# Two recurrent layers of attention and routed experts: the shared experts of layer 0 in weight-stationary chunks, half of them beside the first projections

## The reference, cut to what matters

```python
x = L0_attn_x                                 # (4, 256, 256) float32: 1024 tokens, 8 tiles of 128
xn = _layernorm(x)
s = _L0_attn_ref(xn, ...)                     # differential attention, 16 heads x 2 maps
g = _silu(_L0_ffn_ref(xn, ...))
x = x + s * g
xn = _layernorm(x)
s = _L1_attn_ref(xn, ...)
g = _silu(_L1_ffn_ref(xn, ...))
x = x + s * g

def _L0_ffn_ref(x, gate_w, w1, w2, w3, sw1, sw2, sw3):
    # _swiglu(t, wa, wb, wo): h = silu(t @ wa.T) * (t @ wb.T); return h @ wo.T
    scores = softmax(t @ gate_w.T)            # 16 experts, INTER = 176
    weights, indices = top_k(scores, 2)
    for e in range(16):
        y = y + _swiglu(t, w1[e], w3[e], w2[e]) * w_e[:, None]
    z = _swiglu(t, sw1, sw3, sw2)             # shared experts, 2 x 176 wide, for every token
    return y + z
```

## Time and profile before

| | |
|---|---|
| median of 3 runs | 543.9 us (542.84 to 544.36) |
| profiled execution: its time, its span | 546.77 us, 545.0 us |
| TensorE busy | 440.9 us, 81% of the span |
| VectorE busy | 325.9 us, 60% |
| ScalarE, GpSimd busy | 188.7 and 184.8 us |
| mean granted TensorE clock | 0.902 |
| layer 0 attention, experts of layer 0, layer 1 | about 0 to 228, 228 to 350, 350 to 545 us |

### The profile page before, as it was taken

The page is one execution under the profiler, slowest core; times in us unless marked ns, Lnnn a source line. Parts: engine busy times, 40 slices in busy tenths (PEclk is TensorE's granted clock), DMA queues, the critical chain, the costliest instruction groups (busy, mean ns, idle before and its releaser), DMA issues.

```text
span 545.0 us, 10275 instructions
## 1 busy us (share of the span) xinstructions
PE 440.9 (81%) x3600; PEld 305.3 (56%) x3600; DVE 325.9 (60%) x831; ACT 188.7 (35%) x407; POOL 184.8 (34%) x224
## 2 busy tenths in 40 slices
PE   3456898878898998799999999765594969889960
PEld 2324666544574564477776776553573646577640
DVE  3786647799887765135331338788569566732335
ACT  1101324443444555633453323121103333454212
POOL 2333200353786214004000047243606385411324
PEclk9857979999999999999999999889567989899985
DMA  7340775466496520413332253033623747000114
GB/s 230 95 122 2 232 225 164 139 200 200 124 292 192 158 55 3 135 60 98 108 106 70 77 188 102 10 92 112 176 86 100 220 150 229 27 2 14 62 34 144
DMA packets 50492, 65.87 MB, mean 121 GB/s; under 512 B 8051, under 2 KB 41715, under 8 KB 48907
## 3 DMA queue, kind: packets, MB, share of 16 engines
q1 hardware_dynamic: 48139, 58.93, 35.5%
q0 software_dynamic: 2304, 6.29, 3.6%
HBM read 42.88 MB, written 22.02 MB: 119 GB/s over the span
## 4 chain that ended last, share of the span: by engine, by line
PE 54%; DVE 21%; POOL 7%; issue 6%; DMA 5%; SPq 3%; ACT 2%; POOLq 0%; DVEq 0%; ACTq 0%
PE bank L1010 9%; PE bank L1032 7%; PE bank L905 4%; DVE work L1471 4%; PE bank L912 4%; PE bank L808 3%; PE bank L839 3%; DMA work<-work 3%; PE bank L955 3%; PE bank L933 3%; PE bank L835 3%; POOL x_slots L1297 2%; DVE work L1435 2%; PE bank L793 2%; PE bank L1017 2%
## 5 line engine op out<-in xcount | busy, mean ns | idle before, releaser
L1471 DVE TENSOR_REDUCE work<-bank 128x4 f32<-128x512 f32 (+1 forms) x144 | 96.3, 687 | 61.1 <-PE bank L839 59.2
L1133 ACT ACTIVATE work<-bank 128x512 f32<-128x512 f32 x144 | 84.1, 595 | 105.7 <-PE bank L863 61.8
L835 PE MATMUL bank<-neg_ts,identb 128*128 128x512 bf16 (+1 forms) x144 | 49.2, 341 | 30.8 <-DVE work L1471 24.5
L1097 ACT ACTIVATE work<-bank 128x256 f32<-128x256 f32 (+4 forms) x131 | 51.5, 401 | 60.3 <-PE bank L905 20.7
L1261 POOL TENSOR_TENSOR work<-work 128x512 f32<-128x512 f32 (+1 forms) x20 | 21.3, 1064 | 109.4 <-ACT work L1097 109.2
L912 PE MATMUL bank<-work,cst 128*32 128x256 f32 (+1 forms) x768 | 52.7, 345 | 0.0
L905 PE MATMUL bank<-work 128*32 128x128 f32 (+1 forms) x704 | 49.0, 352 | 3.9 <-POOL work L1252 2.6
L1774 DVE TENSOR_TENSOR work<-work,bank 128x176 f32<-128x176 f32 x47 | 15.8, 336 | 59.6 <-ACT work L1186 59.3
L839 PE MATMUL bank<-work 96*128 96x256 bf16 (+1 forms) x320 | 50.2, 262 | 0.0
L1032 PE MATMUL bank<-moe,work 88*128 (+1 forms) x188 | 50.2, 390 | 0.0
L1010 PE MATMUL bank<-moe,work 128*128 x124 | 42.1, 462 | 0.8 <-ACT work L1097 0.5
(11 more groups left out here) (196 smaller groups left out, 772.9 us busy)
## 6 DMA issues: line engine op xcount, KB each, us to landing
moe<-w_in SPq DMA_DIRECT2D x27, 352.0 KB, 3.9
work<-q_parts SPq DMA_DIRECT2D x48, 128.0 KB, 2.6
x_slots<-wo SPq DMA_DIRECT2D x9, 512.0 KB, 3.9
work<-x_slots SPq DMA_DIRECT2D x31, 128.0 KB, 2.2
y_slots<-work SPq DMA_DIRECT2D x31, 128.0 KB, 1.7
q_parts<-work SPq DMA_DIRECT2D x8, 384.0 KB, 2.7
parts<-work SPq DMA_DIRECT2D x8, 384.0 KB, 2.8
moe<-parts SPq DMA_DIRECT2D x24, 128.0 KB, 2.6
```

Source lines behind the costliest of these rows:

```text
L835: nc.tensor.matmul(view[:, :, half * P:half * P + P], identb[:, :], neg_ts[:, :].unsqueeze(1).to_broadcast([P, len(ms), P]), start=True, s ...
L1097: return nc.scalar.activation(dst, src, ACT.Copy)
L1133: nc.scalar.activation(pT[at % 6], a.st.bank(w)[:, :], ACT.Exp, scale=SCALE)\
L1471: nc.vector.tensor_reduce(here[:, first:first + len(ms), half], a.s.bank((b, q))[:, :].rearrange("p (m s) -> p m s", s=n), AX_X, ALU.max, ...
```

## The change

The shared experts become chunks of work on a pair of tiles (256 tokens). Chunk c of pair g is one half (88 of 176 columns) of one shared expert: TensorE multiplies with the weights as the stationary operand (`shared_up`: 4 products of 256 columns, first and third matrix side by side in one PSUM bank), ScalarE takes the silu of one half of the bank, VectorE multiplies it by the other, and the result, already turned, is the stationary operand of `shared_down` (2 products of 256 columns), which adds up all four chunks of a pair in one bank. The transposes of the hidden rows, the copies of them, and the adds into `acc` go away for the shared experts; ScalarE copies the finished bank.

Pairs 0 and 1 (`AHEAD = 2`, tiles 0 to 3) are put on layer 0's line of beats: pair 0 at beats 7 to 13, pair 1 at beats 18 to 27, with PSUM banks 4 to 7 that the exponentials need later. Their results are stored to a DRAM tensor (`shared0`) and loaded into `acc` during the third routed tile. The shared weights are loaded at the start, behind the masks and ahead of the second half of x, and leave the bulk list (35 loads instead of 38); the first bulk load of `w2` waits for both stores, as the parked results use its place. Pairs 2 and 3 remain in the expert loop as 8 rounds (31 to 38). The loop has 50 rounds instead of 53, the combinations stand in rounds 37 to 44, and layer 1's first steps start at round 42 instead of 44. The silu of the gate is written in place (`acc` for `gval`), and some loads share a semaphore.

```diff
+         bulk=(30, 2), shared=(((7, 8, 9), (8, 9, 10), (9, 10, 11), (10, 11, 12), 13),
+                                ((18, 19, 20), (20, 21, 22), (22, 23, 24), (24, 25, 26), 27)),
...
-         early=(44, 0, 3, 4, 4, 5, 9, 9, 10)),
+         early=(42, 0, 3, 4, 4, 5, 9, 9, 10)),
...
+CHUNKS = 2 * SHARED
+COMBINE = (6, 7, 8, 9, 10, 11, 12, 13)
+ROUNDS0 = 50
...
+            for g, at in enumerate(c.get("shared", ())):
+                for k, (up, hidden, down) in enumerate(at[0:CHUNKS]):
+                    put(up, "shared_up", CHUNKS * g + k)
+                    put(hidden, "shared_hidden", CHUNKS * g + k)
+                    put(down, "shared_down", CHUNKS * g + k)
+                put(at[CHUNKS], "shared_out", g)
...
+        sh.up = Ring(banks[4:7], sem("sh_up_full"), dve=sem("sh_hidden"))
+        sh.bank = banks[7]
...
-            return [t for t in range(TILES) if max(SLOT_TILES0 + 7 + t, SLOT_TILES0 + 4 + 2 * t) + lag == n]
+            return [t for t, at in enumerate(COMBINE) if SLOT_TILES0 + at + lag == n]
...
-        N0 = SLOT_TILES0 + SHARED * TILES
+        N0 = SLOT_TILES0 + CHUNKS * (TILES // 2 - AHEAD)
...
             sp.dma_start(masks, consts_d[:, C_KEPT:C_TABLES]).then_inc(ld["cst"], 16)
+            sp.dma_start(w13[:, E0:], w13_d[:, E0:]).then_inc(ld["shared"], 16)
+            sp.dma_start(w2[0:FH, E0:], w2_d[:, E0:]).then_inc(ld["shared"], 16)
             for g in range(2, TILES // 2):
                 x_pair(g)
...
+                    elif kind == "shared_out":
+                        sp.wait_ge(sh.out, w + 1)
+                        sp.dma_start(shared_d[w * SEQ:(w + 1) * SEQ, :].rearrange("(t p) d -> p t d", p=P),
+                                     early_out.rearrange("p (t d) -> p t d", d=D)).then_inc(sh.kept, 16)
...
                 if n == 3:
                     sp.dma_start(x_again, x_d.rearrange("(t p) d -> p t d", p=P)).then_inc(ld["x2"], 16)
+                    sp.dma_start(acc[:, 0:2 * AHEAD, :], shared_d.rearrange("(t p) d -> p t d", p=P)).then_inc(ld["x2"], 16)
...
+                if a.n == 0 and key == (0, 0, 0):
+                    sh.up.wait_drained(pe)
+                    pe.wait_ge(sh.out, AHEAD)
...
+            def shared_up(bank, k):
+                g, c = divmod(k, CHUNKS)
+                part, f = divmod(c, 2)
+                for u in range(2):
+                    col = u * F0 + f * FH
+                    for d in range(KD):
+                        mm = nc.tensor.matmul(bank[0:FH, u * SEQ:(u + 1) * SEQ], w13[:, E0 + part, d, col:col + FH],
+                                              xnT[:, d, 2 * g:2 * g + 2, :], start=(d == 0), stop=(d == KD - 1))
+                return mm
+
+            def shared_down(bank, hidden, k):
+                part, f = divmod(k % CHUNKS, 2)
+                for u in range(2):
+                    mm = nc.tensor.matmul(bank[:, u * D:(u + 1) * D], hidden[0:FH, k % 3, u * P:(u + 1) * P],
+                                          w2[0:FH, E0 + part, f, :], start=(k % CHUNKS == 0 and u == 0),
+                                          stop=(k % CHUNKS == CHUNKS - 1), skip_group_check=True)
+                mm.then_inc(sh.down, 1)
...
+                    elif kind == "shared_up":
+                        if w == 0:
+                            pe.wait_ge(ld["shared"], 32)
+                        pe.wait_ge(*a.pj.emptied(("x", w // CHUNKS)))
+                        sh.up.wait_free(pe, w)
+                        shared_up(sh.up.bank(w), w).then_inc(sh.up.full, 1)
+                    elif kind == "shared_down":
+                        if w % CHUNKS == 0 and w:
+                            pe.wait_ge(sh.out, w // CHUNKS)
+                        pe.wait_ge(*sh.up.emptied(w))
+                        shared_down(sh.bank, early_hidden, w)
...
+            def shared_silu(bank, hidden, k):
+                if k >= 3:
+                    act.wait_ge(sh.down, k - 2)
+                nc.scalar.activation(hidden[0:FH, k % 3, :], bank[0:FH, 0:SEQ], ACT.Silu).then_inc(sh.silu, 1)
...
+                    elif kind == "shared_out":
+                        if w:
+                            act.wait_ge(sh.kept, 16 * w)
+                        act.wait_ge(sh.down, CHUNKS * (w + 1))
+                        copy(early_out, sh.bank[:, :]).then_inc(sh.out, 1)
...
+            def shared_hidden(ring, key, hidden, k):
+                dve.wait_ge(sh.silu, k + 1)
+                half = hidden[0:FH, k % 3, :]
+                nc.vector.tensor_tensor(half, half, ring.bank(key)[0:FH, SEQ:2 * SEQ], ALU.mult).then_inc(ring.free["dve"], 1)
...
-                    if j < SLOT_TILES0:
-                        if j >= 4:
-
-                            dve.wait_ge(ys_stored[j % 4], 16 * (j // 4))
-                        nc.vector.tensor_copy(ys[:, j % 4, :], src).then_inc(m0.dn.free["dve"], 1)
-                    else:
-                        t, part = divmod(j - SLOT_TILES0, SHARED)
-                        if part == 0:
-                            nc.vector.tensor_copy(acc[:, t, :], src).then_inc(m0.dn.free["dve"], 1)
-                        else:
-                            dve.wait_ge(*m0.dn.emptied(j - 1))
-                            nc.vector.tensor_tensor(acc[:, t, :], src, acc[:, t, :], ALU.add).then_inc(m0.dn.free["dve"], 1)
+                    if j >= 4:
+
+                        dve.wait_ge(ys_stored[j % 4], 16 * (j // 4))
+                    nc.vector.tensor_copy(ys[:, j % 4, :], m0.dn.bank(j)[:, 0:D]).then_inc(m0.dn.free["dve"], 1)
```

165 lines of the change are left out of this document (98 added, 67 removed).

## The result

The changed kernel takes 553.3 us (median; 551.95 to 556.18) against 544.1 for the kernel before in the same session: ratio 1.0158, 95% interval 1.0121 to 1.0194. Run again in a later session, beside e9, e11 and e12, it was 1.0115 (1.0041 to 1.0189). The forecast was 542.5 with a range of 536.5 to 549.0: it missed, in sign too. The profiled execution took 551.95 (span 550.1), 5.2 above the profiled one of before (546.77).

The account below looks back on a forecast made before the run. TensorE was taken to bound the late expert stage, VectorE the time after 345 us. The terms -9.3 + 1.2 + 7.0 + 0.5 - 0.8 = -1.4 us took the median 543.9 to 542.5, range 536.5 to 549.0.

Parts of the forecast that it names:

- The late stage, -9.3: Late experts to layer 1's first row maximum: removed shared rounds and waits bring that maximum 9.3 us sooner, at 376.9.
- Its cold projections: Late stage: idle TensorE starts layer 1's transposes and first projection at the low clock, a new wait of +3.0 us.
- Pair 0, +1.2: Layer 0, beats 7 to 13: VectorE's multiplies and a silu wait delay the first row maximum 1.2 us, to 34.75.
- Pair 1, +7.0: Layer 0's row maxima, beats 18 to 27: TensorE's strict order delays batch 1's first turn by 7.0 us more, to 52.7.
- clock, +0.5: Layer 0's row maxima: TensorE's clock may relapse after a thin stretch; one relapse costs 1.7 us, taken as +0.5.
- rival 1: Layer 0: row maxima take pair 1 in back to back, +3.4 us for all early cost, total 537.2; chance 0.15.
- Loads, -0.8: Three fewer bulk loads end before the fourth batch's maxima rows, which land faster: 0.8 us saved, bounds 0 and -1.1.
- Acc fetch, table loads, parked rows: 0: Fetching parked results during the third routed tile and ScalarE's table switches beside layer 0's exponentials are covered: 0 us.
- rival 5: ScalarE among layer 0's row maxima: a silu comes late behind its table loads; chance 0.03.
- The signs listed beforehand: Observations that would confirm the forecast: TensorE without early hole, landmark times in both layers, granted clock near 1.
- rival 4: Layer 1's first steps: VectorE and GpSimd contend more, only 6.4 us come back late, total 545.4; chance 0.08.
- bound of -7.1: Late stage: the smallest gain the forecast allowed, 7.1 us, beside -15 as the largest.

Follow-up runs that it names:

- e9: Changed kernel with half-size fillers (unused TensorE products in the late stage) and the last normalisation ahead of the second projections' turns: ratio 0.9986 to the kernel before.
- e11: Changed kernel with no pair early, all sixteen shared chunks in the expert loop, last normalisation moved ahead, second batch's rows four rounds later: ratio 1.0030 to the kernel before.
- e12: Changed kernel with pair 1's four down products one beat later: ratio 1.0016 to the kernel before.
- e6: Changed kernel with the last two tiles' normalisation ahead of the second projections' turns on VectorE: ratio 1.0050 to the kernel before.
- e5: Changed kernel with half-size fillers (18, 15 and 9 unused TensorE products) in the late stage's idle stretches: ratio 1.0062 to the kernel before.
- e14: Changed kernel with pair 1's downs one beat later, the last normalisation moved ahead and half-size late fillers of TensorE: ratio 0.9880 to the kernel before.
- e2: Changed kernel without pair 1's four early chunks, rows of x standing in for their results: ratio 1.0002 to the kernel before.
- e1: Changed kernel without any early chunk, rows of x standing in for the parked results: ratio 0.9952 to the kernel before.
- e13: Changed kernel with pair 1's downs one beat later and the last normalisation ahead of the second projections' turns: ratio 0.9933 to the kernel before.
- e15: Changed kernel with both pairs' downs one beat later and the last normalisation ahead of the second projections' turns: ratio 0.9917 to the kernel before.
- e10: The changed kernel, unaltered, run again in a later session: ratio 1.0115 to the kernel before.
- e18: The kernel before, unaltered, run once more for a second trace: layer 1's first row maximum at 388.08 us, against 386.17 in its first trace.

## Why the prediction was wrong, point by point

- **The late stage, -9.3: this step failed.** It gave 2.6 in the profiled pair, and 2.6 to 4.9 over the traces. The first half of it held: the gathers gate the first norm, which ended 1.1 us later relative to the first expert round (0.8 forecast). What failed is the stretch behind it: 38.1 us, where the sum said 34.0 and I took 31.8. By rows: VectorE waits 5.8 us for projections (the sum left 3.0), and the last normalisation takes 4.5 beside GpSimd (1.5 in the operations of before). Together that is 5.8 us more, of which some 1.7 net came back elsewhere: the waits for GpSimd's powers (1.2 in the earlier trace rows) are gone and fewer combinations and gates meet GpSimd, but a second normalisation meets it too (3.1 us from 368.47 on). The other 2.2 were the choice of the lower of two sums "as the groups count overlapped ends twice". I had added up "with as much contention as those of before show", and the normalisations among those, three in the earlier trace rows, ran without company; the one at 28.50 in the same trace had it. An operation's company is a property of when it runs, and the change moved it. e6 shows it: with the normalisation out of that company and inside a wait, the stretch is 33.4, between the two sums.
- **Its cold projections.** The forecast had them (+3.0) and gave them to the first projection only; the second ones ran cold as well (TensorE idle 8.0 us before the second pair's transposes and 5.7 before its projections). e5 gets part of the second wait, e14 nothing more: it is one wait, which either a warm clock or other work of VectorE fills. The first wait stays at 3 us in all of them.
- **Pair 0, +1.2:** 1.4 at the first maximum in the changed kernel's trace (0.5 to 2.4 over all kernels with pair 0 early), and 2.7 in time (e2 against e1). Mis-sized: the wait for the last silu was named but not priced apart, and there was no term for the clock behind a pair that is done early (0.50 from 37.0 to 47.2 in e2). What moves the first maximum by over a microsecond between versions with the same pair 0 is open.
- **Pair 1, +7.0:** 7.7 at the turn, 6.2 to 8.5 in time, so the walk through the order was right, with TensorE's two waits of 0.77 us and the three ups, downs and products as listed. (Layer 0 as a whole, 7.9 in the forecast, is 8.3 in this pair of traces but 7.9 to 10.9 over all of them, so the close agreement is in part luck.) The **clock, +0.5,** was one relapse at 38.8 to 42.2, just where the text put it: 3.4 us at a granted clock of 0.50, so 1.7 lost, and the weight was too small. (The 1.7 us that the forecast gave one relapse rest on no row of the kernel before. Its trace has the clock at 0.50 for 3.4 us from 175.5 on, but also for 20.5 from 21.9 on, and e2 for 10.2: that the run showed just 1.7 is luck.) What the walk didn't ask is whether the price belongs to the work or to its order; the lower bound that it named (turn at 47.9, rival 1) is a beat away (48.95 in e12).
- **Loads, -0.8:** e1, which keeps the changed order of loads, has its turn 0.60 us later than before and its first expert round 0.79 later (229.43 against 228.64): no gain that reaches the experts.
- **Acc fetch, table loads, parked rows: 0.** Held. In ScalarE's timeline of the kernel after, the table loads between silu 5 and 6 took 1.28 us each, the exponential began 0.02 behind the first, and no multiply waited for them. Silu 6 began at 47.60, 1.10 behind the second load and released by TensorE, so the case of rival 5 (0.03), a silu late behind its tables, did not come:

```profile
43.70 1.28 ACT L1196 ACT_TABLE_LOAD   x1
45.00 0.20 ACT L1196 ACTIVATE small<-small 128x2 f32<-128x2 f32 x1
45.22 1.28 ACT L1176 ACT_TABLE_LOAD   x1
```

- **The signs listed beforehand.** No hole of TensorE from 16 to 30: held, though narrowly (e13 and e15, with the same loads, wait 0.31 and 0.95 us for the shared weights there). First maximum near 34.8 (34.97), gathers 0.8 later relative to the experts (1.3), turn near 53 (54.89): near. Clock near 1 from 39 to 55: 0.50 up to 42.2, then 1.00. Layer 1's first maximum 9 us sooner relative to the experts: 2.6. Sooner by 6 was the sign of rival 4, contention of VectorE and GpSimd as the steps close up. It named the right mechanism, at 0.08, and less than half of the shortfall (2.9 of 6.7); the bound of -7.1 on the late term was no bound, since it held contention at the level of before.
- **A count in parentheses.** For a pair of tiles the forecast set 6,144 columns against 5,888 of the old rounds. In passes, as it counts elsewhere, they are 12,288 and 10,752: the new form costs TensorE 10.3 us for a pair where the old one cost 9.0. No other number rests on it.
- **What stays open.** The profiled executions differ by 5.2 us, the medians by 9.1 at first and by 6.7 (ratio 1.0115) later. The changed kernel's median is the same in both sessions (553.3 and 553.2); that of before was 544.1, from four executions, and 545.1 to 546.5, from 13 to 31, in all later sessions. So part of the first 9.1 lies in those four. The steps above explain the profiled pairs (5.1 us of span at first, 5.4 for e10 against e18); where the rest lies no run shows.

## What to carry to other kernels

When work leaves an engine, sum the engine that stays, operation by operation and with its neighbours at their new times: here VectorE took seven times as long for a small step beside GpSimd (1.11 us against 0.16), and moving one normalisation was worth as much as the work that left. When work is put among the steps of a chain, ask what the order alone costs, by giving every product one more step before its consumer: here one beat was worth as much as six of the eight us that the work seemed to cost. Here the freed engine also ran at a lower clock (0.68 against 0.84 in the last stretch); try filling the waits that this causes with other work before warming it.

## What the runs showed of the hardware

Steps of VectorE on 128x2 elements that ran 0.16 us alone took 1.07 and 1.11 in the kernel after beside GpSimd's operations and ended with them to 0.02 us; one of before, at 28.50, took 1.02 and did the same. Row maxima that read PSUM did not slow down (1.27 us for two beside GpSimd in e6, 1.28 alone at 36.20 in the kernel before).

The granted clock of TensorE reads 0.50 or 1.00 in all twenty traces, in stretches of 3.4 us or multiples of that, but for the last of each. It read 0.50 at the first projections in e5 (357.4 to 360.7), where TensorE had been busy 7.1 of the 10.3 us before but only 0.8 of the last 4.0, and from 37.0 to 47.2 in e2 behind 3.9 us with 0.28 busy. In the kernel before, 512 columns of bf16 took 0.43 us at 0.50 (32.59 to 33.02) and 0.22 at 1.00 (43.50 to 43.72), which is 1.2 and 2.3 columns a ns. A product of 128x256 fp32 operands ran as two passes of 0.22 us (e5: 36 in 7.93 us).
